# A graph attention pass: the destination rows x_r are turned to the edges by three bf16 products on exact parts of x_r, with bf16 one-hots, in place of one 4-byte product

## The reference

```python
x_l = (x @ W_l.T + b_l).reshape(n, H, C)
x_r = (x @ W_r.T + b_r).reshape(n, H, C)
z = jax.nn.leaky_relu(x_l[src] + x_r[dst], NEG_SLOPE)
e = jnp.einsum('ehc,hc->eh', z, att)
m = jax.ops.segment_max(e, dst, num_segments=n)
e = jnp.exp(e - m[dst])
denom = jax.ops.segment_sum(e, dst, num_segments=n)
alpha = e / (denom[dst] + 1e-16)
out = jax.ops.segment_sum(alpha[:, :, None] * x_l[src], dst, num_segments=n)
```

## Time and profile before

| | us |
|---|---|
| median of 3 runs | 2293.53 |
| lowest and highest run | 2286.96, 2294.94 |
| the profiled execution | 2275.89 |
| its span, first to last instruction | 2274.1 |
| around the span | 1.8 |
| PE, DVE, ACT and POOL busy in the span | 1739.4, 1806.4, 1108.3, 859.3 |

### The profile page before, as it was taken

The page is one execution under the profiler, slowest core; times in us unless marked ns, Lnnn a source line. Parts: engine busy times, 40 slices in busy tenths (PEclk is TensorE's granted clock), DMA queues, the critical chain, the costliest instruction groups (busy, mean ns, idle before and its releaser), DMA issues.

```text
span 2274.1 us, 38102 instructions
## 1 busy us (share of the span) xinstructions
PE 1739.4 (76%) x8653; PEld 1332.9 (59%) x8653; DVE 1806.4 (79%) x5400; ACT 1108.3 (49%) x2824; POOL 859.3 (38%) x861
## 2 busy tenths in 40 slices
PE   2677777998999999645688888788738788878876
PEld 1322224877888887333577778678725555555554
DVE  7988887899899895777777878886387777778775
ACT  0666665887887784210234334334334544444443
POOL 2000000000000000057777777771017777777771
PEclk7755567999999999766587677765557878787888
DMA  4255555765665675055656666652112222222221
GB/s 150 106 152 156 152 150 168 291 229 198 238 242 214 242 260 205 0 163 151 176 162 187 169 167 185 170 168 76 36 40 54 55 54 54 55 55 55 56 56 42
DMA packets 192476, 314.96 MB, mean 139 GB/s; under 512 B 25873, under 2 KB 139416, under 8 KB 182418
## 3 DMA queue, kind: packets, MB, share of 16 engines
q1 hardware_dynamic: 163312, 248.12, 33.4%
q0 software_dynamic: 27712, 63.56, 10.8%
q10 hardware_dynamic: 1250, 0.86, 0.1%
HBM read 232.38 MB, written 80.07 MB: 137 GB/s over the span
## 4 chain that ended last, share of the span: by engine, by line
POOL 24%; PE 19%; issue 12%; DVE 6%; DMA 3%; ACT 1%; DVEq 0%; POOLq 0%; SPq 0%; ACTq 0%
POOL G L682 12%; POOL G L667 8%; POOL SCR L667 4%; PE PS L1881 4%; PE PS L1777 3%; PE PS L1737 3%; PE PS L1987 2%; PE PS L1857 1%; DMA G<-table,src_idx 1%; PE PS L1882 1%; DMA gathered_rows<-G 1%; PE PS L1962 1%; DVE RX L925 1%; ACT HB L699 1%; PE PS L1833 1%
## 5 line engine op out<-in xcount | busy, mean ns | idle before, releaser
L667 POOL DMA_INDIRECT G<-table,src_idx x252 | 264.3, 1049 | 988.7 <-DMA table<-RX 910.4
L682 POOL DMA_INDIRECT G<-table,gather_idx x415 | 408.9, 985 | 277.2 <-DMA table<-RX 151.1
L1987 PE MATMUL PS<-SCR,OH 128*128 128x256 f32 x830 | 284.0, 507 | 109.4 <-DVE SCR L1624 109.2
L1987 PEld LDWEIGHTS PS<-SCR,OH 128*128 128x128 f32 x830 | 203.0, 254 | 162.3 <-DVE SCR L1624 122.0
L1777 PE MATMUL PS<-ALL_R 128*128 128x256 f32 (+3 forms) x2025 | 266.7, 289 | 19.5 <-DVE ALL_R L1216 9.0
L1857 PE MATMUL PS<-RX,OH 128*128 x830 | 187.5, 390 | 120.7 <-DVE SCR L1324 68.6
L1777 PEld LDWEIGHTS PS<-ALL_R 128*128 128x128 f32 (+1 forms) x2025 | 251.5, 191 | 22.5 <-DVE ALL_R L1216 9.4
L1881 PE MATMUL PS<-AT 128*128 128x128 f32 x830 | 252.6, 400 | 15.1 <-issue 7.6
L1857 PEld LDWEIGHTS PS<-RX,OH 128*128 128x128 f32 x830 | 159.0, 271 | 146.0 <-issue 142.7
L830 ACT ACTIVATE AT<-iota,EI 128x128 f32<-128x128 f32 x415 | 132.2, 389 | 194.8 <-PE PS L1882 191.3
L1725 PE MATMUL PS<-AT,G 128*128 128x400 bf16 x474 | 173.4, 495 | 64.2 <-DVE AT L1109 44.8
(11 more groups left out here) (392 smaller groups left out, 3370.8 us busy)
## 6 DMA issues: line engine op xcount, KB each, us to landing
ALL_R<-adjacency SPq DMA_DIRECT2D x72, 1600.0 KB, 6.8
adjacency<-ALL_R SPq DMA_DIRECT2D x26, 1600.0 KB, 7.4
AT<-gathered_rows SPq DMA_DIRECT2D x103, 256.0 KB, 3.7
gathered_rows<-G SPq DMA_DIRECT2D x63, 256.0 KB, 2.7
AT<-dst_in_block SPq DMA_DIRECT2D x103, 128.0 KB, 3.9
gathered_rows<-SCR SPq DMA_DIRECT2D x40, 256.0 KB, 2.3
G<-table,gather_idx POOLq DMA_INDIRECT x415
G<-table,src_idx POOLq DMA_INDIRECT x252
```

What stands on the lines that cost most here:

```text
L667: pool.indirect_dma_start(score_rows(i)[:, q], None, tables[0], bass.IndirectOffsetOnAxis(ap=src_idx[:, v:v + 1], axis=0)).then_inc(s(f"sc ...
L682: pool.indirect_dma_start(G[:, p, q, :], None, tables[i], bass.IndirectOffsetOnAxis(ap=gather_idx[:, p, q:q + 1], axis=0)).then_inc(s(f"{n ...
L1987: ins = pe.matmul(PS[:, q, 0:MSG], OH[:, p, q, :], view(SCR, M_AT + (p * VB + q) * MSG, [[1, MSG]]), start=True, stop=True)
```

## The change

x_r is held as three bf16 arrays whose sum is x_r. ACT casts it to `XR_HIGH` once it is complete. DVE subtracts that from x_r and leaves the rest in `H`. ACT casts the rest to the first half of `XR_PARTS`, and DVE subtracts again and writes what is left, as bf16, to its second half. The one-hots of the score pass are bf16 and lie in `Z_HOTS`. For each visit PE makes three bf16 products with the same one-hot, which add up in the same place of PSUM. `score_inputs` takes the place of `sum_words_made`; PE and the sums' one-hots on ACT wait for it. The new arrays lie where `RX`, `OH` and `means` have room, and no other buffer moves.

```diff
@@ act, after the copies of x_r @@
+            act.wait_ge(s("xr_copied"), 7)
+            act.copy(XR_HIGH[:, 0:NPAD], view(RX, 0, [[1, NPAD]])).then_inc(s("xr_copied"), 1)
+            act.wait_ge(s("score_inputs"), 1)
+            act.copy(XR_PARTS[:, 0:NPAD], H[:].rearrange("p b d -> p (b d)")).then_inc(s("xr_copied"), 1)
...
-            act.wait_ge(s("sum_words_made"), 1)
+            act.wait_ge(s("score_inputs"), 2)
@@ dve, after the self scores @@
+            rest = H[:].rearrange("p b d -> p (b d)")
+            dve.wait_ge(s("xr_copied"), 8)
+            dve.tensor_tensor(rest, view(RX, 0, [[1, NPAD]]), XR_HIGH[:, 0:NPAD], ALU.subtract).then_inc(s("score_inputs"), 1)
@@ dve, hot_by_dst @@
-                dve.tensor_scalar(view(OH, k % DEPTH * VB * P, [[1, w]]), near(k % DEPTH)[:, 0:w], tv[:, 0, 0:1], None, ALU.is_equal).then_inc(s("z_hot"), 1)
+                dve.tensor_scalar(Z_HOTS[:, k % DEPTH * SB * P:k % DEPTH * SB * P + w], near(k % DEPTH)[:, 0:w], tv[:, 0, 0:1], None, ALU.is_equal).then_inc(s("z_hot"), 1)
@@ dve, before the pass @@
             pack_words()
+            dve.wait_ge(s("xr_copied"), 9)
+            dve.tensor_tensor(XR_PARTS[:, NPAD:2 * NPAD], rest, XR_PARTS[:, 0:NPAD], ALU.subtract).then_inc(s("score_inputs"), 1)
+            dve.wait_ge(s("score_inputs"), 3)
             list_ends()
@@ pe, turned @@
                     b = (word >> (5 * q)) & 31
-                    ins = pe.matmul(view(PS, Z_PS + q * P, [[1, P]]), view(OH, (k % DEPTH * VB + q) * P, [[1, P]]),
-                                    view(RX, b * D, [[1, D]]), start=True, stop=True)
+                    hot = Z_HOTS[:, (k % DEPTH * SB + q) * P:(k % DEPTH * SB + q + 1) * P]
+                    pe.matmul(view(PS, Z_PS + q * P, [[1, P]]), hot, view(XR_HIGH, b * D, [[1, D]]), start=True, stop=False)
+                    pe.matmul(view(PS, Z_PS + q * P, [[1, P]]), hot, view(XR_PARTS, b * D, [[1, D]]), start=False, stop=False)
+                    ins = pe.matmul(view(PS, Z_PS + q * P, [[1, P]]), hot, view(XR_PARTS, b * D + NPAD, [[1, D]]), start=False, stop=True)
...
-            pe.wait_ge(s("sum_words_made"), 1)
+            pe.wait_ge(s("score_inputs"), 3)
```

More of the change, by code:

```diff
@@ L128, in gnn_program @@
         HT_AT = NV * 8 + NPAD + 136
+        with nc.sbuf_tensor("XR_PARTS", [P, NPAD + 32 * D], BF16) as XR_PARTS:
+            pass
         RX = place("RX", [P, HT_AT + 2 * NV * HEADS + 80])
@@ L139, in gnn_program @@
         G = place("G", [P, DEPTH, VB, D])
+        with nc.sbuf_tensor("XR_HIGH", [P, 32 * D], BF16) as XR_HIGH:
+            pass
         OH = place("OH", [P, DEPTH, VB, P])
@@ L165, in gnn_program @@
         self_prob = sb("self_prob", [P, NBLK, HEADS])
+        with nc.sbuf_tensor("Z_HOTS", [P, DEPTH * SB * P], BF16) as Z_HOTS:
+            pass
         means = sb("means", [P, NBLK, 32])
@@ L1384, in pack_words @@
                     done(dve.tensor_tensor(word, word, shifted, ALU.bitwise_or))
-                dve.memset(small[:, 6, :], 0.0).then_inc(s("sum_words_made"), 1)
+                dve.memset(small[:, 6, :], 0.0).then_inc(s("score_inputs"), 1)
             def scan_visits(i):
```

## The result

The changed kernel takes 2360.35 us (median of six executions, 2352.74 to 2362.12) where the kernel before takes 2288.34 us beside it (six, 2283.53 to 2294.94): a ratio of 1.0311, 95% interval 1.0286 to 1.0336. It is 72 us slower. Against the span before that is 85.9 us more; the profile before was of an execution 12.5 us faster than the median, so I read places and sizes from the profiles and the price from the medians.

The account below looks back on a forecast made before the run. POOL's gathers bound the pass, PE's issue just under them; 6 + 1 + 27 + 11 - 2 = +43, plus 3 for double sets at half clock, +46 on 2293.5, 2339.5, said as 2340 us; range 2304 to 2362.

Parts of the forecast that it names:

- almost no room below: In this pass POOL's gathers set the pace, 5.35 us a step, with PE and DVE just under it.
- A register instruction costs 0.097 us, a visit 0.57: PE's sequencer: five register instructions and three products make a visit 0.57 us against 0.32, a step 1.0 us longer.
- 1 + 27 + 11 = 39: Issue terms in us: steps 25 to 33 +1, three groups in steps 34 to 81 +27, steps 82 to 103 +11.
- This is issue time, the same at either clock.: PE's step: the 1.0 us of longer issue does not depend on whether the clock is full or half.
- the 7.3 and 5.0 of the forecast: PE's sequencer time per step: 7.3 us with eight visits of sums, 5.0 with four; before, 6.3 and 4.0.
- The clock falls too: Rival, chance 0.12: less array work keeps the clock at half in catch-up stretches, +6 to +15 on top, 2346 to 2355.
- Groups +9 each: Each 16-step group in steps 34 to 81: nine steps with sums +6.7, three covered by DVE 0, four around transposes +2.4.
- +2.4: Four steps around a group's transposes, where PE and DVE alternate: 0.6 us each, +2.4 a group.
- Steps 82 to 103, +11: 22 steps already behind POOL: six covered by DVE, half the rest at 1.0 us, half at 0.4, +11.
- After step 103, 0: After the pass's step 103 only sums remain, with unchanged instructions, so no cost.
- The start, +6, first product at about 1004: Before the first products: added DVE passes and ACT casts, 8.1 us less a 2.10 wait, +6; L1874's first at about 1004.
- What would have shown me wrong: Signs against: visits 0.32 to 0.4 apart, POOL never waiting after step 5, steps with four visits of sums under 4.5 us.

Follow-up runs that it names:

- b_fixed: Kernel before with the block of x_r fixed at build, so a visit's three register instructions are gone and the output differs: 2287.72 us, ratio 1.0003.
- b_reg2: Kernel before with two more register instructions in each visit, giving the same block, and nothing else changed: 2333.52 us, ratio 1.0189.
- a_filler: Changed kernel with one more 4-byte 128 x 128 product per visit, on constant operands, overwritten afterwards: 2335 us, ratio 1.0204, of three executions.
- a_fixed_parts: Changed kernel with middle and low products at blocks fixed at build: three products, three register instructions a visit, output differs: 2314.14 us, ratio 1.0105.
- a_one_product: Changed kernel with only the product on the high part; middle and low parts are made but not added: 2299.65 us, ratio 1.0059.
- a_one_lean: Changed kernel with only the high-part product, and without the two subtractions and second cast that make the other parts: 2293.44 us, ratio 1.0008.
- a_one_reg2_again: Changed kernel with only the high-part product and two more register instructions a visit, second set of runs: 2342.27 us against 2291.32, ratio 1.0222.
- b_issue: Kernel before with two tiny products (4 rows by 8 columns) ahead of each 4-byte product, five register instructions a visit: 2481.47 us, ratio 1.0842.

## Why the prediction was right, and where it was off

The forecast was slower, 2340 us in a range of 2304 to 2362; it is 2360, 1.6 us inside the upper end. As a difference it was +46 in +31 to +71, and is +72: the mechanism is the forecast one, its size was too small by about a third. Step by step:

- **The kernel before has "almost no room below" the gathers' pace.** Right. b_fixed and b_reg2 show the edge from both sides, 0 us for three register instructions fewer and 45 for two more.
- **A register instruction costs 0.097 us, a visit 0.57.** Right: 0.57 measured where nothing is queued, and 5.10 and 7.52 us a step at full clock in a_filler. b_reg2 has about three quarters of the added issue (2 x 0.097 of the 0.25 us a visit) and costs 45 us. Of the forecast's issue terms, 1 + 27 + 11 = 39, that share is 30. So the price of one instruction was right and the sum over the steps too small.
- **"This is issue time, the same at either clock."** It looks wrong in the adds and is right in the queue. At half clock the adds of single steps are 4.61 us apart and that of step 74 comes 8.44 after the one before (1430.32 to 1438.76), not 5.0 and 7.3. But the sequencer loads the word for a step's products (L1864) at this pace, from step 73's products to step 74's, and from there over three more steps:

```profile
L1864 PEldq TENSOR_LOAD <-low_sums x2: 297/302/306, 1426.9 to 1434.3; - x2
...
L1864 PEldq TENSOR_LOAD <-low_sums x4: 297/302/656, 1434.3 to 1449.2; - x4
```

  That is 7.4 us, and 4.97 for each of three: the 7.3 and 5.0 of the forecast. The four adds sum to 8.44 + 3 x 4.61 = 22.3, and so does the queue. The array alone needs less: a_fixed_parts, with the same products and two register instructions fewer, has 21.9 for the same four steps at clock 0.50 (adds at 1396.49 and 1418.36). In the double step the array falls behind the queue, in the single ones it catches up at its own 4.61, and every fourth step it stands still for the queue, here and again 0.57 us at 1452.81:

```profile
1430.38 0.50 PEld L1899 LDWEIGHTS PS<-AT 128*128 128x128 f32 x2 [0.42 <-issue]
```

  So a step's time alone would name the array, and the sum over four steps names the queue. At half clock the two are only 2% apart. Steps 73 to 81, seven single and two double, took 50.3 us (1425.47 to 1475.72) where I had 49.6.
- **"The clock falls too" was a rival at 0.12, worth +6 to +15.** It happened. It was no separate case but came on top. I priced it in the double steps; what a_filler shows is a gain in the steps around the transposes. a_filler, with more work but a higher clock, is 25 us faster than the changed kernel. The other way: changed kernel less b_reg2 is 2360.35 - 2333.52 = 27 us; 6 are the start, 21 are left for the lower clock and the issue of two more products a visit. How these 21 divide no run shows.
- **Groups +9 each.** Measured 12.0 and 13.0; b_reg2 alone has +9.3 and +8.7. The nine steps 73 to 81 cost +7.3 where I had +6.7. The undersized term is the seven steps 66 to 72, "+2.4": they take 47.8 us where they took 42.2, +5.6 (steps 50 to 56: +5.9), and b_reg2 has +2.8 and +4.9 there. How much of the rest is the clock no run shows.
- **Steps 82 to 103, +11.** The worst-sized term: +29.5. Even b_reg2 has 160.6 - 138.9 = +21.7 there. I let DVE cover six steps and gave half of the rest 0.4 us. The three longest steps, 82, 90 and 98, each three steps behind a group's last, make 13.5 of the 29.5, far more than 1.0 us of issue each. Nor is issue all of it: a_one_product, with the old issue at half clock, takes 150.1 us there, +11.2. That PE comes from a wait there, with its issue on the path and its clock at half, fits both; no run takes the two apart.
- **After step 103, 0.** Measured +7.5 of the profiles, 6.2 of them in the sums, whose instructions are the same. They ran at 0.57 before and at 0.50 now, but at 0.50 they ran in b_fixed too, which takes the time of the kernel before (stretches of the sums before, in b_fixed and after):

```profile
1566.00:1640.00 74.00, 66.18 (x347) 65.57 (x346) 25.66 (x64) 33.97 (x92) 0.00 (x0) 0.57 0.20 55
...
1570.00:1650.00 80.00, 73.91 (x347) 72.88 (x346) 25.65 (x64) 34.29 (x92) 0.00 (x0) 0.50 0.18 51
...
1645.00:1725.00 80.00, 73.64 (x345) 72.62 (x344) 25.23 (x64) 34.20 (x92) 0.00 (x0) 0.50 0.18 50
```

  b_reg2, a_one_product and a_one_lean need the same 80 us. So the 6 us may be a gain of the one profiled execution before, which was 12.5 us faster than the median, and no cost of the change; that would be part of why the profiles differ by 85.9 us and the medians by 72.
- **The start, +6, first product at about 1004.** Right in size: 5.8 in the profile and 6.2 between a_one_product and a_one_lean. The product came at 1007.1, since 3.5 us had been lost before the change's first instruction.
- **What would have shown me wrong**: visits 0.32 to 0.4 apart, POOL never waiting, steps with four visits of sums under 4.5 us. The first did occur, and I was not wrong by it: in the steps with sums the visits start 0.32 us apart at the weight loads (1437.39, 1437.71 and 1438.03 in step 74), and the twelve products take 1.3 us, not 2.2 to 2.5. Work queued behind the sums reaches the array bunched, so the spacing there says nothing of the queue's pace; a visit every 0.57 us shows only where nothing is queued. The third was near, with 4.61. POOL's waits went to 68.7 us where I said 30 or more. PE's busy time rose instead of falling, from 70.8 to 86.5 us in the group: at half clock the sums last longer.

The sum by the profiles: 3.5 us before the change's first instruction, 6.3 for the start (the add of step 0 comes at 1022.41, 9.8 later than before), 1.2 for steps 1 to 33 (11.0 later at step 33), 37.9 for the three groups to step 81, 29.5 and 7.5: 85.9.

## What to carry to other kernels

Count what the sequencer has to do per matmul, the address arithmetic above all, and not only the array's passes: here three cheap products with five register instructions lost to one costly product with three. When an engine that isn't the bound stands just under it, try the change in both directions (a little less work, a little more); that tells the edge in two runs. Read the queue's pace from the queue (its word loads) and over several steps: the time of one step can be the array's while the sum is the queue's. And a product made lighter can lower the granted clock for everything beside it, so reckon its neighbours at half clock too.

## What the runs showed of the hardware

- Two more register instructions a visit on PE (830 in all) cost 45 us in b_reg2 and 40 to 43 in a_one_reg2_again, 0.05 us each of the whole time; start to start one takes 0.097.
- In b_issue the weight load of a 4-byte product of 4 rows by 8 columns started only 0.07 us before the product ahead of it ended, after 0.23 us of idle weight loads. Two of them, whose loads take 0.14 us, made a visit of 0.91 us out of one of 0.427 in the array. A small product isn't a cheap one among large ones.
- The granted clock stayed at 0.50 from 1430.4 to 1452.2 of the changed kernel, where weight loads followed each other without a gap; in a_filler, with a 4-byte product beside the bf16 ones, it was 0.87 over 16 steps. A run that held the clock apart from the work was not made.
